# Two graph layers gather rows and sum them on TensorE: table rows stored as three bf16 parts, each sum made of three bf16 matmuls

## The chip, the cores and the metric

The kernel runs on 1 core of a Trainium2 chip. The metric is the device time of one launch in microseconds (us), lower is better. Engines: TensorE (PE; its weight loads are listed apart as PEld), VectorE (DVE), ScalarE (ACT), GpSimd (POOL), and SyncE (SP), which here issues DMAs and passes semaphores on. Each engine runs its own instruction stream in order; they meet at semaphores.

## What is computed

One layer of a graph network with 6250 nodes of 256 features and 100000 edges (sorted by `dst`), then a linear attention and a mixture of experts:

```python
xn = _layernorm(x)
# twice (W1, then W2): for every edge a row of the source node is added to the row of dst
xw  = x @ W
out = segment_sum(xw[src] * (dis[src] * dis[dst])[:, None], dst) + b   # plus the node's own row
h   = elu(out)
x = x + gnn(xn) + linear_attention(xn)
x = x + moe(_layernorm(x))           # 8 experts, top 2
```

The norm is split: a table in DRAM holds `dis[src] * row`, so that a sum over edges is a sum of table rows, scaled by `dis[dst]` afterwards.

## The kernel before, in words

The program is a row of phases with a barrier between them; each builds its own instruction streams, unrolled. Those that matter here:

- **prep** (to about 92 us). At its end 49 tiles of 128 nodes are scaled by DVE (`SCALE_V`) and ACT (`SCALE_A`) into `acc`, and SP writes them to DRAM, `table[0]`, in 7 chunks of 7 tiles.
- **l0** and **l1**, one for each graph layer. 782 tiles of 128 sorted edges meet 49 tiles of 128 destination nodes in 833 **steps**; a step is one tile of edges against one tile of nodes. `gathers` on POOL issues one indirect DMA for each tile of edges (128 table rows of 256 floats, 1 KB each) into a ring `rows` of 32 slots. `tiles_here` on SP waits for a tile's landing, raises `here`, then waits until the tile 16 places earlier has been summed (`summed`) and raises `freed`, for which POOL waits when its ring is full. `four_selects` on DVE makes 0/1 matrices for four steps at once. `step_sum` on PE multiplies one such matrix with the slot's rows into one of 4 PSUM banks, and `step_add` on DVE adds the bank to `acc`. PE may be 4 steps ahead of DVE's adds (`PSB`). Per 4 steps PE and DVE each load four words (tile counts, block offsets) into registers. Between the steps, `between(i, k)` puts other work in 49 rounds of 16 steps: the projections and context of the attention in l0, its output and the splitting of the expert weights in l1.
- **c0**, between l0 and l1: 25 pairs of node tiles are transposed, multiplied with W1 and passed through elu; POOL scales the result into `acc`, and SP writes each pair to `table[1]`. `slots` runs a software pipeline in which slot n does another stage for pair n, n-1, n-2.
- after l1: the second conv, the router, and the expert phase from about 2645 us, in which PE is busy over 90% of the time.

Of the kernel before, what the change touches and what calls it, by code (L numbers as in the profile page):

```python
# [14 lines left out]
P = 128  # L15
# [11 lines left out]
DX = D + 4  # L27
CODE = 1 << 13
# [30 lines left out]
XCH = 7  # L59
# [10 lines left out]
def gps_layer(nc, x, src, dst, wqkv, wproj, bproj, gw1, gb1, gw2, gb2, wr, br, wide, vectors, out):  # L70
# [37 lines left out]
    table = [dram(f"rows_layer{i}", [n * P, D], F32) for i, n in enumerate((NT, 2 * PAIRS))]  # L108
# [16 lines left out]
    with whole, nc.allow_non_contiguous_dma("a few columns of one word"):  # L125
# [231 lines left out]
        with ExitStack() as ph:  # L357
# [3 lines left out]
            before = sb(ph, "before", [P, SG, SG * P], BF16)  # L361
# [4 lines left out]
            rows_i = sb(ph, "rows_i", [P, 2, SG, P], I32)  # L366
            rows_b = sb(ph, "rows_b", [P, SG, P], BF16)
            rows_f = sb(ph, "rows_f", [P, SG, P])
            z_i = sb(ph, "z_i", [P, STEPS - 1], I32)
            hi_i = sb(ph, "hi_i0", [P, STEPS - 1], I32)  # L370
            lo_b = sb(ph, "lo_b", [P, STEPS - 1], BF16)
            hi_b = sb(ph, "hi_b", [P, STEPS - 1], BF16)
            hi_hot = sb(ph, "hi_hot", [P, HI, STEPS - 1], BF16)
# [3 lines left out]
            cnt_s = sb(ph, "cnt_s", [P, SCOL, GP], BF16)  # L377
# [15 lines left out]
            SCALE_V, SCALE_A = (0, 2, 4, 6), (1, 3, 5)  # L393
# [7 lines left out]
            with nc.Block() as block:  # L401
                @block.sync
                def _(sp):
# [28 lines left out]
                    for c in range(XIN):  # L432
                        sp.wait_ge(sem("scaled_v"), (c + 1) * len(SCALE_V))
                        sp.wait_ge(sem("scaled_a"), (c + 1) * len(SCALE_A))
                        sp.dma_start(table[0][c * XCH * P:(c + 1) * XCH * P, :].rearrange("(t p) d -> p t d", p=P),
                                     accv[:, c * XCH:(c + 1) * XCH, :]).then_inc(sem("tab0"), 16)
                    sp.wait_ge(sem("tab0"), XIN * 16)

                @block.gpsimd
                def _(pool):  # L440
                    pool.wait_ge(sem("copy_d"), 32)
                    for g in range(SG):
                        pool.wait_ge(sem("t_i"), g + 1)
                        at = bass.IndirectOffsetOnAxis(ap=t_i[:, g:g + 1], axis=0)
                        pool.indirect_dma_start(rows_i[:, 0, g, :], None, e_dst_rows, at).then_inc(sem("rows_d"), 16)
                    pool.wait_ge(sem("counted"), 2)
                    pool.memset(acc[:, NT * D:BLOCKS * D], 0.0).then_inc(sem("acc_tail"), 1)

                @block.vector
                def _(v):  # L450
# [92 lines left out]
                    v.wait_ge(sem("by"), 2)  # L543
                    for c in range(XIN):
                        for k in SCALE_V:
                            i = c * XCH + k
                            v.tensor_scalar(accv[:, i, :], node[:, i, :], by_x[:, i:i + 1], by_1[:, i:i + 1], ALU.mult, ALU.add
                                            ).then_inc(sem("scaled_v"), 1)

# [54 lines left out]
                def _(a):  # L604
# [22 lines left out]
                    a.activation(deg[:, :], ps_deg, ACT.Sqrt, bias=ones[:, 0:1]).then_inc(sem("std"), 1)  # L627
                    a.wait_ge(sem("by"), 2)
                    for c in range(XIN):
                        for k in SCALE_A:  # L630
                            i = c * XCH + k
                            a.activation(accv[:, i, :], node[:, i, :], ACT.Identity, scale=by_x[:, i:i + 1], bias=by_1[:, i:i + 1]
                                         ).then_inc(sem("scaled_a"), 1)

# [299 lines left out]
        with ExitStack() as ph:  # L934
            ctx_name[0] = "c0"
            work = sb(ph, "work0", [P, 10, 2 * D])
            sc, aggt, zz, ez, hh = conv_views(work)
            bk = banks(ph, 5)
            ps_t, ps_z, ps_m = bk[0:2], bk[2:4], bk[4]
            with nc.Block() as block:  # L940
                @block.sync
                def _(sp):
                    def body(n, q, has):
                        if has(2):
                            sp.wait_ge(sem("c_u0"), n - 1)
                            sp.dma_start(table[1][bass.ds((n - 2) * 2 * P, 2 * P), :].rearrange("(h p) d -> p h d", p=P),
                                         pair(accv, n - 2)).then_inc(sem("tab1"), 16)
                    slots(sp, body)
                    sp.wait_ge(sem("tab1"), PAIRS * 16)

                @block.gpsimd
                def _(pool):
# [6 lines left out]
                    slots(pool, body)  # L959
# [11 lines left out]
                def _(a):  # L971
                    a.wait_ge(sem("ctx_w"), 1)
                    a.activation(ctx_q[:, :, :].rearrange("p c o -> p (c o)"), ps_m[:, :], ACT.Copy).then_inc(sem("ctx_s"), 1)
                    conv_scalar(a, 0)

                @block.vector
                def _(v):
                    slots(v, lambda n, q, has: conv_vector(v, 0, n, q, has))


        with ExitStack() as ph:
            ctx_name[0] = "l1"
            rows = sb(ph, "rows1", [P, ROWS, D])
            rows_flat = rows[:, :, :].rearrange("p r d -> p (r d)")
            sel = sb(ph, "sel1", [P, SELS, P])
# [698 lines left out]
```

## Time and profile before

| | |
|---|---|
| device time, median of 3 runs | 3353.7 us (3351.02 to 3356.55) |
| span of the profiled execution | 3317.0 us |
| prep's table write ends, first gather of l0 | about 92 us, 93.9 us |
| steps of l0 (first to last add) | 98.0 to 1257 us |
| c0 | about 1258 to 1323 us |
| steps of l1 | 1331 to 2487 us |
| PE / DVE / ACT / POOL busy | 71% / 53% / 19% / 59% of the span |

The span runs from the first to the last instruction on the core; the device time has some 37 us more around it (3353.7 - 3317.0, if the profiled execution was a usual one). Times inside the trace are counted from the span's start. The spans of PE records are modelled, so what PE has really finished is read from the engines that wait for it.

### The profile page before, as it was taken

How to read it: one execution, taken by the hardware profiler on the slowest of the kernel's cores; microseconds unless marked ns; L12 is line 12 of the kernel's file. 1: busy time of each engine (PE TensorE's matmuls, PEld its weight loads, DVE VectorE, ACT ScalarE, POOL GpSimd, SP SyncE). 2: the span in 40 equal slices, each digit the busy share in tenths (PEclk: the TensorE clock that was granted, in tenths of full speed). 3: DMA queues.
4: the chain of work that ended last, by engine and by line, in shares of the span. 5: the costliest groups of instructions: out<-in, count | busy, mean ns of one | idle time of the engine just before them, and what ended most of it. 6: DMA issues, size and time to landing. Idle time of an engine off the chain costs nothing. (4 is left out here: it accounts for less than half of the span.)

```text
span 3317.0 us, 45225 instructions
## 1 busy us (share of the span) xinstructions
PE 2369.2 (71%) x10847; PEld 1754.6 (53%) x10847; DVE 1747.8 (53%) x4268; ACT 619.3 (19%) x1318; POOL 1965.4 (59%) x2107
## 2 busy tenths in 40 slices
PE   3366766666776678356666566666669499999998
PEld 2244444444444446234444344434448399999997
DVE  6144444444444456245444455555556666676666
ACT  2000000000000005000000011110006444444443
POOL 1566666666666653766666666666644155555554
PEclk9777888888877879677777877787789599999999
DMA  6333333333333322444444445444431455555551
GB/s 170 114 94 88 93 90 90 92 91 92 89 93 88 89 77 80 122 138 139 141 147 140 140 146 148 146 145 144 144 92 63 170 185 148 148 148 151 148 149 20
DMA packets 177902, 397.25 MB, mean 120 GB/s; under 512 B 42393, under 2 KB 96570, under 8 KB 169514
## 3 DMA queue, kind: packets, MB, share of 16 engines
q0 software_dynamic: 96800, 233.29, 26.7%
q1 hardware_dynamic: 50926, 103.38, 8.7%
q10 hardware_dynamic: 30012, 58.67, 5.2%
q8 instruction: 68, 1.11, 0.1%
q14 instruction: 96, 0.79, 0.1%
HBM read 322.87 MB, written 75.01 MB: 120 GB/s over the span
## 5 line engine op out<-in xcount | busy, mean ns | idle before, releaser
L644 POOL DMA_INDIRECT rows<-rows_layer,srcs x1564 | 1538.3, 984 | 762.3 <-issue 382.0
L705 PE MATMUL l_bank<-rows,sel 128*128 x3332 | 1191.5, 487 | 638.8 <-issue 246.1
L695 DVE TENSOR_TENSOR acc<-acc,l_bank 128x256 f32 x1666 | 698.9, 419 | 1233.1 <-remote 546.7
L705 PEld LDWEIGHTS l_bank<-rows,sel 128*128 128x128 f32 x3332 | 700.3, 235 | 1013.3 <-issue 482.7
L1638 PE MATMUL ps_y<-whl,hhi 128*128 128x512 f32 x896 | 320.8, 398 | 0.0
L1594 POOL DMA_INDIRECT out<-ys,g_sum x112 | 179.9, 1606 | 200.5 <-DVE ys L1550 175.2
L673 DVE TENSOR_TENSOR sel<-iota_n,dloc 128x512 f32<-128x512 f32 x418 | 286.4, 686 | 20.1 <-issue 20.1
L1509 ACT ACTIVATE hr<-ffn_bank,vec 128x256 f32<-128x256 f32 x448 | 212.7, 475 | 374.2 <-PE ffn_bank L1450 336.8
L1448 PE MATMUL ffn_bank<-xh,whl 128*128 128x256 f32 x896 | 252.2, 281 | 2.4 <-DVE xl L1524 2.4
L1449 PE MATMUL ffn_bank<-xl,whl 128*128 128x256 f32 x896 | 252.0, 281 | 0.0
L1450 PE MATMUL ffn_bank<-xh,whl 128*128 128x256 f32 x896 | 251.9, 281 | 0.0
L1640 PE MATMUL ps_y<-whl,hlo 128*128 128x256 f32 x896 | 250.0, 279 | 0.0
L1533 DVE TENSOR_TENSOR hlo<-hr,hhi 128x256 fp32r<-128x256 f32 x448 | 191.1, 427 | 15.4
L830 PE MATMUL l_bank<-w_qkv,xt 128*128 128x512 f32 (+1 forms) x392 | 172.2, 591 | 37.3 <-issue 31.5
L1638 PEld LDWEIGHTS ps_y<-whl,hhi 128*128 128x128 f32 x896 | 168.0, 188 | 37.6
L1448 PEld LDWEIGHTS ffn_bank<-xh,whl 128*128 128x128 f32 x896 | 169.6, 189 | 5.2 <-DVE xl L1524 2.8
L1450 PEld LDWEIGHTS ffn_bank<-xh,whl 128*128 128x128 f32 x896 | 169.6, 189 | 0.0
L1449 PEld LDWEIGHTS ffn_bank<-xl,whl 128*128 128x128 f32 x896 | 169.4, 189 | 0.0
L1640 PEld LDWEIGHTS ps_y<-whl,hlo 128*128 128x128 f32 x896 | 168.1, 188 | 0.0
L1565 POOL DMA_INDIRECT xr<-rows_x,g_row x112 | 115.9, 1034 | 63.2 <-POOL g_row L1561 44.4
L830 PEld LDWEIGHTS l_bank<-w_qkv,xt 128*128 128x128 f32 x392 | 88.9, 232 | 120.1 <-issue 105.9
L768 ACT ACTIVATE xt<-l_bank 128x256 f32<-128x256 f32 x49 | 18.8, 383 | 644.3 <-remote 420.0
(273 smaller groups left out, 2208.3 us busy)
## 6 DMA issues: line engine op xcount, KB each, us to landing
whl<-w_hi SPq DMA_DIRECT2D x32, 1024.0 KB
whl<-w_lo SPq DMA_DIRECT2D x32, 1024.0 KB
rows<-rows_layer,srcs POOLq DMA_INDIRECT x1564
w_qkv<-wide ACTq DMA_DIRECT2D x49, 335.0 KB
w_hi<-whi ACTq DMA_DIRECT2D x49, 335.0 KB
w_lo<-wlo ACTq DMA_DIRECT2D x49, 335.0 KB
rows_layer<-acc SPq DMA_DIRECT2D x25, 256.0 KB, 2.1
rows_x<-acc SPq DMA_DIRECT2D x7, 910.0 KB
```

Source lines behind the costliest of these rows:

```text
L644: pool.indirect_dma_start(rows[:, (n + 1) % ROWS, :], None, table[layer], bass.IndirectOffsetOnAxis(ap=srcs[:, n:n + 1], axis=0)).then_inc ...
L673: v.tensor_tensor(sel[:, s % SELS:s % SELS + FOUR, :], iota_n[:, None, :].to_broadcast([P, FOUR, P]), dloc[:, s:s + FOUR, None].to_broadca ...
L695: v.tensor_tensor(to, to, step_bank(s), ALU.add).wait_op(sem(f"summed{layer}"), s + 1, "sem-ge").then_inc(sem(f"added{layer}"), 1)
L705: t.matmul(step_bank(s), sel[:, s % SELS, :], rows_flat[:, bass.ds(slot * D, D)], start=True, stop=True).wait_op(sem(f"here{layer}"), t.to ...
L830: ins = t.matmul(to[:, 0:n], xt[:, c, :], w_qkv[:, c, lo:lo + n], start=(c == 0), stop=(c == KC - 1))
L1448: t.matmul(to, a[0], b[0], start=first, stop=False)
L1449: t.matmul(to, a[0], b[1], start=False, stop=False)
L1450: return t.matmul(to, a[1], b[0], start=False, stop=last)
L1509: a.activation(hr[:, m % 4, :], ps_h[m % 4][:, 0:TS], ACT.Gelu, bias=vec[q][:, O_B1 + m:O_B1 + m + 1]).then_inc(sem("e_g"), 1)
L1533: v.tensor_tensor(hl[q][:, m, :], hr[:, m % 4, :], hh[q][:, m, :].bitcast(F32), ALU.subtract).then_inc(sem("e_hs"), 1)
L1638: t.matmul(ps_y[:, h, :, :], hh[q][:, m, h * P:(h + 1) * P], whl[q][:, :, at], start=(m == 0), stop=False)
L1640: ins = t.matmul(ps_y[:, h, 0, :], hl[q][:, m, h * P:(h + 1) * P], wh[q][:, at], start=False, stop=(m == HC - 1))
```

## The change

The table in DRAM no longer holds 256 floats a row but 3 x 256 bf16 values, 1.5 KB: `hi = bf16(row)`, `mid = bf16(row - hi)`, `lo = bf16(row - hi - mid)`. The select matrices are bf16 too, and a step's sum is three accumulating bf16 matmuls. In prep and in c0 the parts are made before each table write: ACT makes `hi` and `mid`, DVE the first remainder, POOL `lo`; three part buffers rotate, each with its own semaphore of the write that reads it, and two buffers of the remainder. Prep's temporary buffers are carved out of one block so that the parts fit, and one tile of seven moves from ACT's to DVE's share of the scaling.

```diff
-    table = [dram(f"rows_layer{i}", [n * P, D], F32) ...
+    table = [dram(f"rows_layer{i}", [n * P, DP], BF16) ...      # DP = 3 * D
@@ step_sum, on PE
-            t.matmul(step_bank(s), sel[:, s % SELS, :], rows_flat[:, bass.ds(slot * D, D)], start=True, stop=True
-                     ).wait_op(sem(f"here{layer}"), t.to_reg(here), "sem-ge").then_inc(sem(f"summed{layer}"), 1)
+            t.matmul(step_bank(s), sel[:, s % SELS, :], rows_flat[:, bass.ds(slot * DP, D)], start=True, stop=False
+                     ).wait_op(sem(f"here{layer}"), t.to_reg(here), "sem-ge")
+            t.matmul(step_bank(s), sel[:, s % SELS, :], rows_flat[:, bass.ds(slot * DP + D, D)], start=False, stop=False)
+            t.matmul(step_bank(s), sel[:, s % SELS, :], rows_flat[:, bass.ds(slot * DP + 2 * D, D)], start=False, stop=True
+                     ).then_inc(sem(f"summed{layer}"), 1)
@@ l0 and l1
-            rows = sb(ph, "rows0", [P, ROWS, D])
-            sel = sb(ph, "sel0", [P, SELS, P])
+            rows = sb(ph, "rows0", [P, ROWS, DP], BF16)
+            sel = sb(ph, "sel0", [P, SELS, P], BF16)
@@ prep, per chunk c of 7 tiles; ACT (its scaling of the chunk comes first)
+                        if c >= 3:
+                            a.wait_ge(sem(f"tab0_{c % 3}"), c // 3 * 16)
+                        a.activation(part[c % 3][:, :, 0, :], accv[:, c * XCH:(c + 1) * XCH, :], ACT.Copy).then_inc(sem("part_hi"), 1)
+                        if c >= 1:
+                            middle(a, c - 1)       # waits rest(c-1), mid = Copy(rest)
@@ prep, DVE and POOL
+                        v.tensor_tensor(rest[c % 2], accv[...], part[c % 3][:, :, 0, :], ALU.subtract)
+                        pool.tensor_tensor(part[c % 3][:, :, 2, :], rest[c % 2], part[c % 3][:, :, 1, :], ALU.subtract)
@@ c0, POOL, slot n (the product of pair n-2 stands ahead of it)
+                        if has(5):
+                            m = n - 5
+                            pool.wait_ge(sem("c_mid"), m + 1)
+                            if m >= 3:
+                                pool.wait_ge(sem(f"tab1_{m % 3}"), m // 3 * 16)
+                            pool.tensor_tensor(part[m % 3][:, :, 2, :], rest[m % 2][:, :, :], part[m % 3][:, :, 1, :], ALU.subtract
+                                               ).then_inc(sem("c_lo"), 1)
@@ c0, ACT, slot n
+                        if has(3):
+                            m = n - 3
+                            a.wait_ge(sem("c_u0"), m + 1)
+                            if m >= 3:
+                                a.wait_ge(sem(f"tab1_{m % 3}"), m // 3 * 16)
+                            a.activation(part[m % 3][:, :, 0, :], pair(accv, m), ACT.Copy).then_inc(sem("c_hi"), 1)
+                        if has(4):
+                            m = n - 4
+                            a.wait_ge(sem("c_r"), m + 1)
+                            a.activation(part[m % 3][:, :, 1, :], rest[m % 2][:, :, :], ACT.Copy).then_inc(sem("c_mid"), 1)
@@ c0, DVE, slot n (after its work for pairs n-1 and n-2)
+                        if has(3):
+                            m = n - 3
+                            v.wait_ge(sem("c_hi"), m + 1)
+                            v.tensor_tensor(rest[m % 2][:, :, :], pair(accv, m), part[m % 3][:, :, 0, :], ALU.subtract
+                                            ).then_inc(sem("c_r"), 1)
```

How the change moves instructions on PE, in the middle of l0's steps. Before, a step is an address computation, its register operation with the wait, and one matmul (`sel` is the select matrix, `rows` the ring):

```order
L700 REGISTER_ALU
L705 ISA
L705 MATMUL l_bank<-rows,sel 128x256
L700 REGISTER_ALU
L705 ISA
L705 MATMUL l_bank<-rows,sel 128x256
```

In the changed kernel at the same place:

```order
L745 REGISTER_ALU
L750 ISA
L750 MATMUL l_bank<-rows,sel 128x256
L752 ISA
L752 MATMUL l_bank<-rows,sel 128x256
L753 ISA
L753 MATMUL l_bank<-rows,sel 128x256
```

A step now has three matmuls, each with a register operation of its own for its offset in the ring; still one address computation and one signal.

ACT in the middle of c0, one slot before (L871 scales the next pair, L880 copies the transposed pair out of PSUM, L884 is the exponential of elu):

```order
L871 ACTIVATE work<-acc,dis 128x256 x2
L880 ACTIVATE work<-c_bank 128x512
L884 ACTIVATE work<-work 128x512
```

One slot of the changed kernel:

```order
L919 ACTIVATE work<-acc,dis 128x256 x2
L928 ACTIVATE work<-c_bank 128x512
L932 ACTIVATE work<-work 128x512
L1039 ACTIVATE part<-acc 128x2x256
L1043 ACTIVATE part<-rest 128x2x256
```

The two part-making copies stand behind the exponential, and ahead of the next slot's scaling.

## Rows read from the trace of the kernel before

**Rows 1.** Groups of instructions on POOL in l0: busy, mean | idle before, by what ended it

```profile
L644 POOL DMA_INDIRECT rows<-rows_layer,srcs x782 | 772.3, 988 | 392.3 <-issue 187.2 <-SPq L666 173.6 <-POOLq L85 31.3
```

**Rows 2.** The same for POOL in l1

```profile
L644 POOL DMA_INDIRECT rows<-rows_layer,srcs x782 | 765.9, 979 | 370.0 <-issue 194.9 <-SPq L666 171.6 <-POOLq L940 3.2
```

**Rows 3.** Who waited for whom, SP's own queue, l0: us, times, longest

```profile
SPq L666 <- PE l_bank L705: 365.4, 288, 5.3
SPq L660 <- DMA rows<-rows_layer,srcs: 8.1, 5, 3.5
```

**Rows 4.** DVE in order of time, first round of l0: start, us, what [idle before]

```profile
117.91 0.42 DVE L695 TENSOR_TENSOR acc<-acc,l_bank 128x256 f32 x1 [3.36 <-remote]
...
122.81 0.42 DVE L695 TENSOR_TENSOR acc<-acc,l_bank 128x256 f32 x1 [3.88 <-remote]
...
158.51 1.53 DVE L695 TENSOR_TENSOR acc<-acc,l_bank 128x256 f32 x3 [17.89 <-remote]
```

**Rows 5.** POOL in order of time, the same stretch

```profile
158.78 0.95 POOL L644 DMA_INDIRECT rows<-rows_layer,srcs  x1 [7.02 <-SPq L666]
```

**Rows 6.** DVE in order of time, a later round of l0

```profile
457.61 0.42 DVE L695 TENSOR_TENSOR acc<-acc,l_bank 128x256 f32 x1 [1.82 <-remote]
460.42 0.42 DVE L695 TENSOR_TENSOR acc<-acc,l_bank 128x256 f32 x1 [2.40 <-remote]
462.63 0.42 DVE L695 TENSOR_TENSOR acc<-acc,l_bank 128x256 f32 x1 [1.78 <-PE l_bank L705]
```

**Rows 7.** POOL in order of time, the same stretch

```profile
462.90 0.95 POOL L644 DMA_INDIRECT rows<-rows_layer,srcs  x1 [2.52 <-SPq L666]
```

**Rows 8.** PE in order of time, the same stretch

```profile
457.17 1.69 PE L705 MATMUL l_bank<-rows,sel 128*128 x6
```

**Rows 9.** DVE in order of time, end of l1, all gathers landed

```profile
2476.16 0.42 DVE L695 TENSOR_TENSOR acc<-acc,l_bank 128x256 f32 x1 [0.69 <-PE l_bank L705]
...
2479.31 0.42 DVE L695 TENSOR_TENSOR acc<-acc,l_bank 128x256 f32 x1 [0.69 <-PE l_bank L705]
```

**Rows 10.** Instructions on the tile rows_i: ns min/median/max, first and last start

```profile
L445 POOL DMA_INDIRECT rows_i<-edges_dst,t_i x7: 952/952/1190, 13.9 to 21.7; - x7
...
L613 ACT ACTIVATE rows_f<-rows_i x1: 827/827/827, 38.1 to 38.1; 128x768 f32<-128x768 int32 x1
```

**Rows 11.** In order of time, the end of prep and the start of l0

```profile
69.80 10.43 ACT L632 ACTIVATE acc<-node,by,by_x 128x256 f32<-128x256 f32 x21 [0.90 <-DVE by L542]
69.80 9.13 DVE L547 TENSOR_SCALAR acc<-node,by_x,by 128x256 f32<-128x256 f32 x28
...
93.88 0.96 POOL L644 DMA_INDIRECT rows<-rows_layer,srcs  x1 [31.27 <-POOLq L85]
```

**Rows 12.** A window of prep: busy of PE, PEld, DVE, ACT, POOL, then PEclk, DMA share, GB/s

```profile
80.00:85.00 5.00, 0.00 (x0) 0.00 (x0) 0.00 (x0) 0.23 (x1) 0.00 (x0) 1.00 1.04 344
```

**Rows 13.** DMA issues of the table writes: KB each, median us to landing

```profile
rows_layer<-acc SPq DMA_DIRECT2D x25, 256.0 KB, 2.1
rows_layer<-acc SPq DMA_DIRECT2D x7, 896.0 KB, 7.9
```

**Rows 14.** In order of time, the middle of c0

```profile
1285.57 1.04 POOL L956 TENSOR_TENSOR acc<-work,dis 128x512 f32<-128x512 f32 x1 [1.13 <-DVE work L925]
...
1286.51 0.42 DVE L922 TENSOR_SCALAR work<-work 128x512 f32<-128x512 f32 x1
...
1286.83 0.62 ACT L884 ACTIVATE work<-work 128x512 f32<-128x512 f32 x1
1286.96 0.69 DVE L925 SCALAR_TENSOR_TENSOR work<-work 128x512 f32<-128x512 f32 x1
1287.35 0.90 ACT L871 ACTIVATE work<-acc,dis 128x256 f32<-128x256 f32 x2
...
1287.73 1.04 POOL L956 TENSOR_TENSOR acc<-work,dis 128x512 f32<-128x512 f32 x1 [1.13 <-DVE work L925]
...
1288.50 0.60 ACT L880 ACTIVATE work<-c_bank 128x512 f32<-128x512 f32 x1 [0.26 <-PE c_bank L896]
```

More of the change, by code:

```diff
@@ L27 @@
 DX = D + 4
+PARTS = 3
+DP = PARTS * D
 CODE = 1 << 13
@@ L107, in gps_layer @@
     tab_d = dram("step_words", [3, SG * P, 2], U16)
-    table = [dram(f"rows_layer{i}", [n * P, D], F32) for i, n in enumerate((NT, 2 * PAIRS))]
+    table = [dram(f"rows_layer{i}", [n * P, DP], BF16) for i, n in enumerate((NT, 2 * PAIRS))]
     rows_x = dram("rows_x", [1 + NT * P, DX], F32)
@@ L376, in gps_layer @@
             hi_flat = hi_hot[:, :, :].rearrange("p h s -> p (h s)")
-            cnt_s = sb(ph, "cnt_s", [P, SCOL, GP], BF16)
+            cnt_s = carve(SCOL * GP).rearrange("p (c g) -> p c g", c=SCOL)
+            part = [prep_mem[:, i * XCH * DP:(i + 1) * XCH * DP].rearrange("p (t k d) -> p t k d", t=XCH, k=PARTS) for i in range(3)]
+            rest = [prep_mem[:, 3 * XCH * DP + i * 2 * XCH * D:3 * XCH * DP + (i + 1) * 2 * XCH * D].bitcast(F32)
+                    .rearrange("p (t d) -> p t d", t=XCH) for i in range(2)]
             cnt_t = sb(ph, "cnt_t", [P, 2, 4, P], BF16)
@@ L447, in _ @@
                     pool.memset(acc[:, NT * D:BLOCKS * D], 0.0).then_inc(sem("acc_tail"), 1)
+                    for c in range(XIN):
+                        pool.wait_ge(sem("rest"), c + 1)
+                        pool.wait_ge(sem("part_mid"), c + 1)
+                        if c >= 3:
+                            pool.wait_ge(sem(f"tab0_{c % 3}"), c // 3 * 16)
+                        pool.tensor_tensor(part[c % 3][:, :, 2, :], rest[c % 2], part[c % 3][:, :, 1, :], ALU.subtract
+                                           ).then_inc(sem("part_lo"), 1)
                 @block.vector
@@ L543, in _, with remainder @@
                     v.wait_ge(sem("by"), 2)
+                    def remainder(v, c):
+                        v.wait_ge(sem("part_hi"), c + 1)
+                        if c >= 2:
+                            v.wait_ge(sem("part_mid"), c - 1)
+                            v.wait_ge(sem("part_lo"), c - 1)
+                        v.tensor_tensor(rest[c % 2], accv[:, c * XCH:(c + 1) * XCH, :], part[c % 3][:, :, 0, :], ALU.subtract
+                                        ).then_inc(sem("rest"), 1)
                     for c in range(XIN):
@@ L627, in _, with middle @@
                     a.activation(deg[:, :], ps_deg, ACT.Sqrt, bias=ones[:, 0:1]).then_inc(sem("std"), 1)
+                    def middle(a, c):
+                        a.wait_ge(sem("rest"), c + 1)
+                        a.activation(part[c % 3][:, :, 1, :], rest[c % 2], ACT.Copy).then_inc(sem("part_mid"), 1)
                     a.wait_ge(sem("by"), 2)
@@ L937, in gps_layer @@
             sc, aggt, zz, ez, hh = conv_views(work)
+            part = [sb(ph, f"part{i}", [P, 2, PARTS, D], BF16) for i in range(3)]
+            rest = [sb(ph, f"rest{i}", [P, 2, D]) for i in range(2)]
             bk = banks(ph, 5)
@@ L942, in _ @@
                 def _(sp):
[L943 to L949, printed above, removed]
+                    for m in range(PAIRS):
+                        sp.wait_ge(sem("c_lo"), m + 1)
+                        sp.wait_ge(sem("c_hi"), m + 1)
+                        sp.wait_ge(sem("c_mid"), m + 1)
+                        sp.dma_start(table[1][m * 2 * P:(m + 1) * 2 * P, :].rearrange("(h p) d -> p h d", p=P),
+                                     part[m % 3][:, :, :, :].rearrange("p h k d -> p h (k d)")).then_inc(sem(f"tab1_{m % 3}"), 16)
+                    for i in range(3):
+                        sp.wait_ge(sem(f"tab1_{i}"), len(range(i, PAIRS, 3)) * 16)
                 @block.gpsimd
```

58 lines of the change are left out of this document (39 added, 19 removed).

## The prediction

> **What bounds the kernel now.** I read the page first, then the groups and waits of the two step phases, then single rounds in order of time. The step phases l0 and l1 hold 2320 of the 3317 us of span. No engine is full in them; POOL is nearest. One gather costs POOL 0.98 to 0.99 us, and its queue adds 0.30 us before the next, so 782 gathers at full pace take 782 x 1.28 = 1003 us, while each phase takes about 1160. What POOL waits for is the rest: of the idle time ended by `freed` and by the queue's own issue (173.6 + 187.2 us in l0, 171.6 + 194.9 in l1) 782 x 0.30 = 235 us is the queue's own, which leaves 126 and 132 us in which the ring was full [rows 1, 2]. The queue of SP says who was late: it waited 365 us for PE's sums and 8 us for landings [rows 3]. So data are always there; it is the sums that come late, and POOL stands still for them.
>
> Why are they late? Not for want of PE's arithmetic. When all gathers are out, four steps take 2479.31 - 2476.16 = 3.15 us, 0.79 us a step [rows 9], well under POOL's 1.28, with DVE's adds, selects and register loads setting the pace. With gathers under way there are two regimes. In one, steps run at that pace. In the other DVE stands idle: adds come 2.8 us apart at 457.61 and 460.42 [rows 6], although PE's record has three sums at 457.17 to 458.86 [rows 8]. In the first round they come 4.9 us apart and then not at all for 18 us, while POOL issues gather after gather; POOL then stops with its ring full, idle for 7.02 us, and at 158.51 three adds run back to back [rows 4, 5]. At 462.63 the same: POOL had stopped 2.52 us before, its last gather (issued at 459.43) had landed, and four waiting sums were signalled at once [rows 6, 7]. In this regime a sum's signal is held up while gathers are in flight, and is let go when the last one has landed. I find such an episode about once a round, near 100 in all; 258 us of waits over 100 is 2.6 us, which is the pause of [rows 7]. What the hold-up is the trace does not say. It says that it isn't the length of the matmul, since sums held for microseconds are let go together.
>
> **The change, part by part.** *The sum itself.* One fp32 matmul goes, three bf16 ones come, each with its register operation. The array time gets shorter, but the fast regime is paced by DVE (worth 0 while the adds wait for DVE's own queue), and in the slow regime the hold-up is per signal, of which there is still one a step. I put the gain of the arithmetic at 0. Its bounds: all the 258 us of waits, plus the tail after the last gather (the steps still owed when the ring is full, about 30 us a phase, of which 7 would stay), 258 + 46 = 304 us gained; below, nothing.
>
> *The gather.* POOL's price does not depend on the bytes: gathers of 128 int32, 0.5 KB a row, took a median of 952 ns, as much as those of 1 KB [rows 1, 10]. So 1.5 KB adds nothing to POOL. The landing gets later by 64 KB. From the table writes (2.1 us at 256 KB, 7.9 at 896) 640 KB cost 5.8 us, which makes 64 KB 0.58 us; from the rate of a full stream, 344 GB/s, it is 0.19 us [rows 12, 13]. An episode ends with the landing of the last gather, so each gets longer by that: 100 x 0.19 to 0.58, 19 to 58 us; I take 30, nearer the lower, since the queue is empty by then. The Trainium skill ("DMA: Bandwidth & Descriptors", Anatomy of one DMA) has a fixed cost of about 2.0 us and bytes over 436 GB/s: 0.15 us more a gather, and an estimate of 15 us in place of my 30. The pause of 2.5 us agrees with its fixed cost.
>
> *PE's sequencer* has two more register operations and two more matmuls a step. Hidden while a step stays under POOL's 1.28 us; where it exceeds DVE's 0.79 it slows the catching up between episodes, and these come closer together. Bounds 0 and 67 us (episodes every 18 us instead of every 23); I take 0 here and keep the rest for the range.
>
> *Prep.* Before, ACT needs 10.43 us and DVE 9.13 for the scaling of all 49 tiles, the DMAs run at 344 GB/s and the first gather starts at 93.88 [rows 11, 12]. Now per chunk: `hi` and `mid` on ACT, 1792 elements each, by the 0.83 us of 768 [rows 10] about 1.7 us; the remainder on DVE about 2.0 (0.42 us for 256 and 0.69 for 512 elements [rows 9, 14], so 1.05 ns an element); `lo` on POOL 3.5 x 1.04 = 3.6 us [rows 14]; the write of 1344 KB 4.0 us at 344 GB/s and 2 us to its signal. Three part buffers rotate, and ACT makes `mid(c)` only after `hi(c+1)`. So from the end of `hi(c+1)`: mid 1.7, lo 3.6, write 6.0, then `hi(c+3)` 1.7: 13.0 us for two chunks. `hi(1)` ends near 76; `hi(3)` 89, `hi(5)` 102, and `hi(6)` follows `write(3)` at 107. Then `mid(6)` at 110, `lo(6)` behind `lo(5)` at 116, the last write at 122, against 92 now: **+30 us**, with 18 as the lower bound (ACT alone, 4.4 us a chunk, no wait for buffers).
>
> *c0.* A pair takes 2.16 us now (1285.57 to 1287.73), with ACT busy for 0.62 + 0.90 + 0.60 of it [rows 14]. Two copies of 0.60 make 3.3 us a pair. But a ring is closed here too. ACT's `hi(n-3)` in slot n waits for the write of pair n-6, whose `lo` POOL makes in slot n-1 behind the product of pair n-3, which in turn waits for DVE and for the exponential in slot n-1. From the end of that exponential: DVE 0.42 + 0.69, product 1.04, `lo` 1.04, the write of 384 KB about 2.5 (2.1 for 256 KB [rows 13]), hand-overs 0.6: 6.3 us to the start of `hi`. From there hi 0.6, mid 0.6, scaling 0.9, copy 0.6 and the next exponential 0.6: 3.3 us. This takes two slots, so a slot takes 4.8 us. Some 22 of 30 slots at 4.8, the others at 2.5 on average: 125 us, against 63: **+60 us**. If writes are signalled early enough the slot is 3.3 us and the sum +33.
>
> *Sum*, on the profiled span: 3317 + 0 (sums) + 30 (landings) + 30 (prep) + 60 (c0) = 3437; with the 36.7 us that lie around it (3353.7 - 3317.0) this is **3474 us**, which I round to 3470. The other phases stay as they are: the expert phase, where PE is full, uses neither table.
>
> **The rivals.** *(a) The hold-up belongs to the fp32 matmuls and goes with them.* For it: I cannot name what holds the signals, and the episodes occur in these two phases, nowhere in c0, where PE's fp32 work runs beside plain DMAs. Against it: as many held sums are let go together as are waiting. Then POOL sets the pace: 3317 - 304 + 90 + 36.7 = 3140 us, and with a tenth left 3170. It decides if more than about 90 of the 258 us of waits go, a third, since that pays for prep and c0. This one ends on the other side. *(b) It goes in part* (half of it): 3317 - 152 + 15 + 90 + 36.7 = 3307. *(c) It gets worse*: if it hangs on the time that gathers occupy the DMA engines, half as many bytes again make it half as long again, 258 x 1.5 = 387, or +129; with the 67 us for a slower catching up, up to 3317 + 129 + 67 + 90 + 36.7 = 3640; I take its middle, 3580. *(d) The rings of three do not bind*, and prep and c0 cost 18 + 33: 3435 with the landings' 30.
>
> **How the numbers follow.** The forecast with (d) as its lower end, 3420 to 3530: 0.45. (a) 0.22, 3120 to 3200. (b) 0.13, 3200 to 3340. (c) 0.16, 3530 to 3640. Near the old time, between (b) and the forecast: 0.04. A measurement of this kernel tells 0.2% (7 us) from no change. Faster: (a) and (b) with a part of the last, 0.36; same 0.02; slower 0.62. The range reaches from 3150, the middle of (a), to 3565, which leaves out a part of (a) and of (c), together under 0.2. The likeliest case's own range is 3420 to 3530.
>
> **What would show it.** Right: `freed` still ends 110 us or more of POOL's true waits in each phase; POOL's mean stays under 1.02 us; rounds with adds 2 to 5 us apart and bursts behind a pause of POOL of 2.7 us or so; the first gather at 120 to 125 us; c0's products on POOL 4.8 us apart. Wrong: if SP waits for landings rather than for PE, and the adds follow the gathers at 1.28 us, (a) holds, and my step "the hold-up is per signal" was false. If the products of c0 are 3.3 us apart, the ring was no limit. If POOL's mean rises with the bytes, each 0.1 us of it costs 156 us, which no case has.

## The result, and the profile after

The changed kernel takes **3489.15 us** (median of 4 runs, 3487.62 to 3490.59), the kernel before 3355.12 us on the same chip (4 runs, 3351.02 to 3356.94): ratio 1.0402, 95% interval 1.0387 to 1.0417. It is slower by 134 us.

The chips of this study differ more than the two kernels do. The kernel before takes 3355 us on the one of this comparison, 3320 us on two others and 3014 to 3017 us on two more. So each ratio below is against the kernel before on the same chip, and for the step phases a row is compared with a row of its own kind of chip. No chip of the experiments was used in two sessions, so "chip" here may as well mean the session on it. The trace of the kernel before that stands ahead of the prediction has a span of 3317.0 us; the executions of that kernel on the two chips of the 3320 us level have 3313 to 3323, so it belongs with them. The first and the last column of the table are of one level, the middle one is not. The last is the run after_again; its profiled execution was the slowest of four, 9 us above their median.

By stage, in us of the trace (the first gather, the last add of a step phase):

| | before | changed, first comparison | changed, a chip of the 3320 level |
|---|---|---|---|
| first gather of l0 | 93.9 | 128.3 | 129.4 |
| l0, first gather to last add | 1163.0 | 1202.6 | 1196.8 |
| c0, to the first gather of l1 | 69.3 | 134.6 | 133.6 |
| l1, first gather to last add | 1160.8 | 1189.9 | 1175.7 |
| rest | 830.0 | 831.0 | 830.5 |
| span | 3317.0 | 3486.4 | 3466.1 |

First the groups of the changed kernel's POOL, l0 and then l1, with the busy time, the mean, and the idle time before by what ended it; they answer to [rows 1, 2].

```profile
L689 POOL DMA_INDIRECT rows<-rows_layer,srcs x782 | 772.2, 988 | 408.3 <-SPq L711 214.0 <-issue 186.6 <-POOLq L87 7.4
L689 POOL DMA_INDIRECT rows<-rows_layer,srcs x782 | 760.6, 973 | 402.9 <-SPq L711 216.0 <-issue 183.1 <-POOLq L990 3.5
```

A gather of 1.5 KB rows costs POOL 988 and 973 ns, as much as one of 1 KB. By the prediction's way of counting (idle ended by `freed` and by issue, less 235 us of the queue's own), 166 + 164 = 330 us are waits for a full ring, against 258 in the trace of before, which is of another level. In after_again, of the same level, they are 313 us, 55 more. (The expectations below take 238 us for the queue, and so have 251 and 323 where this text has 258 and 330.)

SP's own queue in l0, from 120 to 1290 us (us, times, longest), which answers to [rows 3]: the sums are late, as before, and landings are not what it waits for.

```profile
SPq L711 <- PE l_bank L753: 466.3, 256, 8.7
SPq L711 <- remote: 266.3, 83, 8.7
...
SPq L705 <- DMA rows<-rows_layer,srcs: 6.9, 3, 3.8
```

The profiles of chips with waits record only a part of the semaphore events: 5768 landing events of gathers in the trace of before, where 1564 gathers make 16 each, and about all of them in before_again. So who released SP is known in part there, and a wait ended by an unrecorded event may be put down to "remote". SP's own instructions do not hang on that. In l0 of before it stood for 779 us ahead of L666, the wait for a sum, and for 92 us ahead of L660, the wait for a landing; on a chip without waits (before_again) it is 38 and 771. The sums were late.

The page's groups of the three matmuls, and of their first weight load:

```profile
L750 PE MATMUL l_bank<-rows,sel 128*128 x1666 | 578.2, 347 | 722.7 <-SPq L705 319.7
L750 PEld LDWEIGHTS l_bank<-rows,sel 128*128 128x128 bf16 x1666 | 199.3, 120 | 989.8 <-SPq L705 522.5
L752 PE MATMUL l_bank<-rows,sel 128*128 x1666 | 589.3, 354 | 8.9 <-issue 8.8
L753 PE MATMUL l_bank<-rows,sel 128*128 x1666 | 588.5, 353 | 5.5 <-issue 5.5
```

The fp32 matmul stood in the trace as two records a step. The records overlap, so their means do not add up. Counted once, PE was busy with the sums for 573 + 618 us in the two phases of before and for 459 + 543 in those of after_again, 0.72 and 0.60 us a step, although the granted clock over the phases fell from 0.80 and 0.74 to 0.73 and 0.64. The arithmetic did get shorter, by 190 us in all, and the phases still got longer.

The end of prep in order of time (start, us, what, idle before), which answers to [rows 11]. First ACT's high parts:

```profile
88.25 1.70 ACT L675 ACTIVATE prep_mem<-acc 128x1792 bf16<-128x1792 f32 x1 [4.78 <-DMA rows_layer<-prep_mem]
...
101.83 1.70 ACT L675 ACTIVATE prep_mem<-acc 128x1792 bf16<-128x1792 f32 x1 [4.96 <-DMA rows_layer<-prep_mem]
```

DVE's scalings in the same stretch:

```profile
79.30 8.22 DVE L577 TENSOR_SCALAR acc<-node,by_x,by 128x256 f32<-128x256 f32 x5
...
89.38 1.69 DVE L577 TENSOR_SCALAR acc<-node,by_x,by 128x256 f32<-128x256 f32 x5
```

DVE's remainder of the last chunk:

```profile
110.20 5.28 DVE L571 TENSOR_TENSOR prep_mem<-acc,prep_mem 128x1792 f32<-128x1792 f32 x1 [3.57 <-POOL prep_mem L468]
```

POOL's low parts, and the first gather of l0:

```profile
78.28 8.12 POOL L468 TENSOR_TENSOR prep_mem<-prep_mem 128x1792 bf16<-128x1792 f32 x2 [15.11 <-ACT prep_mem L663]
...
117.33 3.57 POOL L468 TENSOR_TENSOR prep_mem<-prep_mem 128x1792 bf16<-128x1792 f32 x1 [3.74 <-issue]
128.26 0.97 POOL L689 DMA_INDIRECT rows<-rows_layer,srcs  x1 [7.35 <-POOLq L87]
```

ACT's high part waits twice, for 4.8 and 5.0 us, for a part buffer's write. Five scalings on DVE take 1.69 us by themselves and 8.22 beside two of POOL's subtractions. The last remainder waits 3.57 us for POOL, since there are two buffers of it, and then takes 5.28 us, against 2.01 where POOL is idle.

The middle of c0 in order of time, which answers to [rows 14]. POOL:

```profile
1396.47 1.04 POOL L1007 TENSOR_TENSOR acc<-work,dis 128x512 f32<-128x512 f32 x1 [2.56 <-DVE work L973]
1397.46 1.15 POOL L1015 TENSOR_TENSOR part<-rest,part 128x512 bf16<-128x512 f32 x1
1401.18 1.04 POOL L1007 TENSOR_TENSOR acc<-work,dis 128x512 f32<-128x512 f32 x1 [2.56 <-DVE work L973]
```

DVE, from the remainder of one pair to the last step of the next:

```profile
1398.75 0.69 DVE L1056 TENSOR_TENSOR rest<-acc,part 128x512 f32<-128x512 f32 x1 [2.36 <-POOL part L1015]
1399.36 0.68 DVE L965 TENSOR_TENSOR work<-c_bank,b_g 128x512 f32<-128x512 f32 x1
1399.96 0.42 DVE L970 TENSOR_SCALAR work<-work 128x512 f32<-128x512 f32 x1
1400.41 0.69 DVE L973 SCALAR_TENSOR_TENSOR work<-work 128x512 f32<-128x512 f32 x1
```

ACT's high part:

```profile
1401.12 0.63 ACT L1039 ACTIVATE part<-acc 128x512 bf16<-128x512 f32 x1 [1.81 <-DMA rows_layer<-part]
```

The products are 1401.18 - 1396.47 = 4.71 us apart (4.54 on average over all 25), against 2.16 before. Two rings are closed here: ACT's high part waits for a part buffer (three of them), and DVE's remainder waits for POOL's low part two pairs back (two rest buffers).

### The profile page after: what moved, and what is told of

It reads as the page before. It is cut to its first block and busy times, and to the rows that moved or that the text cites. A ratio compares the mean times of both kernels' runs of the same rounds, so it can differ in the third digit from the quotient of the medians.

```text
span 3486.4 us, 52130 instructions
## 1 busy us (share of the span) xinstructions
PE 2318.2 (66%) x12513; PEld 1677.3 (48%) x12513; DVE 1795.5 (52%) x4307; ACT 665.9 (19%) x1375; POOL 2016.0 (58%) x2139
## 5 line engine op out<-in xcount | busy, mean ns | idle before, releaser
L750 PE MATMUL l_bank<-rows,sel 128*128 x1666 | 578.2, 347 | 722.7 <-SPq L705 319.7
L750 PEld LDWEIGHTS l_bank<-rows,sel 128*128 128x128 bf16 x1666 | 199.3, 120 | 989.8 <-SPq L705 522.5
L752 PE MATMUL l_bank<-rows,sel 128*128 x1666 | 589.3, 354 | 8.9 <-issue 8.8
L753 PE MATMUL l_bank<-rows,sel 128*128 x1666 | 588.5, 353 | 5.5 <-issue 5.5
L718 DVE TENSOR_TENSOR sel<-iota_n,dloc 128x512 bf16<-128x512 f32 x418 | 286.3, 685 | 19.2 <-issue 19.2
L878 PE MATMUL l_bank<-w_qkv,xt 128*128 128x512 f32 (+1 forms) x392 | 210.9, 701 | 60.2 <-issue 30.5
L752 PEld LDWEIGHTS l_bank<-rows,sel 128*128 128x128 bf16 x1666 | 187.6, 113 | 80.4 <-issue 27.3
L753 PEld LDWEIGHTS l_bank<-rows,sel 128*128 128x128 bf16 x1666 | 192.4, 115 | 68.3 <-issue 9.9
L878 PEld LDWEIGHTS l_bank<-w_qkv,xt 128*128 128x128 f32 x392 | 102.4, 275 | 159.4 <-issue 120.0
L1528 PEld LDWEIGHTS ffn_bank<-xh,whl 128*128 128x128 f32 x896 | 170.2, 190 | 5.2 <-DVE xl L1604 2.8
```

What stands on the lines that cost most here:

```text
L718: v.tensor_tensor(sel[:, s % SELS:s % SELS + FOUR, :], iota_n[:, None, :].to_broadcast([P, FOUR, P]), dloc[:, s:s + FOUR, None].to_broadca ...
L878: ins = t.matmul(to[:, 0:n], xt[:, c, :], w_qkv[:, c, lo:lo + n], start=(c == 0), stop=(c == KC - 1))
L1528: t.matmul(to, a[0], b[0], start=first, stop=False)
```

## The experiments

### The kernel before, profiled again

No edit.

> The kernel before, profiled a second time. The device time of the changed kernel lies 1.7 us above the span of its profile (3488.1 against 3486.4), that of the kernel before 36.7 us above its own (3353.7 against 3317.0). Theory: the profiled execution of before was a quick one, and a second profile has a span of 3340 to 3355, most of the 25 to 35 us in the two step phases. Rival: the gap belongs to this kernel, and the span is again 3315 to 3320.

It ran in 3011.56 us, span 3009.7, on a chip where the kernel before has a median of 3014.16 us (7 runs). Neither theory foresaw a chip 10% quicker. Its POOL in l0 and l1:

```profile
L644 POOL DMA_INDIRECT rows<-rows_layer,srcs x782 | 759.7, 971 | 269.3 <-issue 217.6 <-POOLq L85 31.3 <-SPq L666 20.4
L644 POOL DMA_INDIRECT rows<-rows_layer,srcs x782 | 769.1, 984 | 241.1 <-issue 202.5 <-SPq L666 35.3 <-POOLq L940 3.2
```

Issue and `freed` together are 238 us in either phase, which is the queue's own 235: no wait for a full ring. SP's waits from 200 to 1050 us:

```profile
SPq L660 <- DMA rows<-rows_layer,srcs: 637.0, 579, 3.2
SPq L666 <- PE l_bank L705: 0.3, 1, 0.3
```

Here SP waits for landings and not for sums. The step phases take 1004.2 and 1012.9 us, the 1003 us that the prediction has for 782 gathers at full pace, and all other stages are as in the trace of before (93.3, 68.9, 830.4 us). So the hold-up, 3317 - 3010 = 307 us of this kernel, is there on some chips and not on others. Also, the device time is only 1.9 us over the span of the same execution: nothing like 37 us lies around a span. The first trace must be from a chip of another level than the times beside it.

### One matmul of the three

```diff
-            t.matmul(step_bank(s), sel[...], rows_flat[:, bass.ds(slot * DP, D)], start=True, stop=False
-                     ).wait_op(sem(f"here{layer}"), t.to_reg(here), "sem-ge")
-            t.matmul(... slot * DP + D ..., start=False, stop=False)
-            t.matmul(... slot * DP + 2 * D ..., start=False, stop=True).then_inc(sem(f"summed{layer}"), 1)
+            t.matmul(step_bank(s), sel[...], rows_flat[:, bass.ds(slot * DP, D)], start=True, stop=True
+                     ).wait_op(sem(f"here{layer}"), t.to_reg(here), "sem-ge").then_inc(sem(f"summed{layer}"), 1)
```

> The changed kernel with the first of the three bf16 matmuls alone; the middle and low parts are made, written and gathered as before but left out of the sums. Theory (a step's pace is set by sums being held while gathers are in flight, not by the length of the matmuls): 3470 to 3490, within 20 us of the changed kernel. Rival (the three matmuls, three weight loads and the PE's sequencer set the pace of a step): two matmuls and two weight loads less are 0.5 to 0.9 us per step, so both step phases fall to what GpSimd can gather, 1003 us each, and the time is 3490 - 2 x 160 = 3170.

On the same chip, without waits: 3105.56 us (3101.63 to 3111.09), ratio 1.0307 (1.029 to 1.0325). The step phases take 999.2 and 1011.2 us, POOL's pace. It could not tell the theories apart, so it was repeated:

> The same kernel as one_matmul (middle and low parts left out of the sums), for a chip on which the kernel before takes about 3320 to 3355 us, with waits for a full ring in its step phases. Theory (the waits are a hold-up that hangs on the gathers in flight and not on the matmuls): the waits stay at 280 us or more, ratio to before 1.035 to 1.042. Rival (the hold-up comes with TensorE's load): two thirds of the matmuls gone, most of the waits go, and the ratio falls below 1.0. If the chip is one without the waits (before near 3014 us), the ratio is again 1.03 and nothing is told.

On a chip of the 3320 level (before 3319.64 us): 3396.75 us, ratio 1.0232 (1.0215 to 1.0249). POOL in l0 and l1:

```profile
L689 POOL DMA_INDIRECT rows<-rows_layer,srcs x782 | 774.6, 991 | 360.7 <-issue 206.7 <-SPq L711 139.2 <-remote 7.4
L689 POOL DMA_INDIRECT rows<-rows_layer,srcs x782 | 763.8, 977 | 362.3 <-issue 213.8 <-SPq L711 136.0 <-remote 8.9
```

111 + 115 = 226 us of waits are left (and 16 us more that the profile puts down to "remote"), with one short matmul a step and 1155.7 + 1145.8 us of phases, against 1196.8 + 1175.7 with three. The ratio lies between my two numbers: the hold-up stays, with or without the other two matmuls, but these two cost 41 + 30 = 71 us, where I had expected nothing. The 71 rest on the slowest execution of after_again. The medians of the two kernels are 3458.58 - 3396.75 = 62 us apart, and the phases of six_parts and four_rests, the same in l0 and l1, are 65 and 60 us longer than here: 60 to 71 us.

The granted clock is not what makes the waits: it was 0.63 in l0 and 0.50 in l1 of one_matmul, which has none, and 0.63 and 0.53 here.

### Longer rows with the fp32 matmul

```diff
+DW = D + D // 2
-    table = [dram(..., [n * P, D], F32) ...]
+    table = [dram(..., [n * P, DW], F32) ...]
...
-            rows = sb(ph, "rows0", [P, ROWS, D])
+            rows = sb(ph, "rows0", [P, ROWS, DW])
```

The table is written in two DMAs a chunk, columns 0 to 255 and 256 to 383; the matmul reads the first 256.

> The kernel before (one fp32 matmul, no parts) with table rows of 384 words instead of 256: 1.5 KB per row as in the changed kernel, the last 128 words a copy of the row's first and in no sum. Theory (the 69 us by which the step phases of the changed kernel are longer come from the bytes of a gather): the step phases lengthen by 50 to 70 us in sum, writing the longer rows costs some us more, 3405 to 3435. Rival (they come from the matmuls): 3355 to 3375.

On the chip without waits: 3038.18 us, ratio 1.0075 (1.0058 to 1.0092), of which 12.5 us is the later first gather (105.8), and 10.4 + 1.2 us the phases. The median gather lands 3.1 us after its issue, against 2.8 in before_again, so the bytes do make each landing 0.3 us later (the chips with waits have too few events recorded to say). Again at the level with waits:

> The same kernel as wide_fp32 (rows of 1.5 KB, one fp32 matmul, the last 128 words in no sum), for a chip with the waits. Theory (the additional waits of the changed kernel, 56 to 72 us, come with the bytes of a gather): waits of 300 to 325 us against 251, ratio to before 1.02 to 1.03. Rival (they come with the matmuls): waits of 250 us, ratio 1.007 as on the chip without waits.

3334.80 us against 3319.64, ratio 1.0048 (1.0031 to 1.0065). POOL in l0 and l1:

```profile
L646 POOL DMA_INDIRECT rows<-rows_layer,srcs x782 | 775.2, 991 | 406.6 <-issue 182.7 <-SPq L668 180.1 <-POOLq L86 42.9
L646 POOL DMA_INDIRECT rows<-rows_layer,srcs x782 | 762.0, 974 | 376.1 <-issue 198.0 <-SPq L668 173.3 <-POOLq L942 3.9
```

128 + 136 = 264 us of waits, 6 more than in the trace of before; the phases take 1165.9 and 1160.1 us, +2.9 and -0.7. The rival holds: the phases are not measurably longer for half as many bytes again.

### Rows of the high part alone

```diff
-    table = [dram(..., [n * P, DP], BF16) ...]
+    table = [dram(..., [n * P, D], BF16) ...]
...
-                                     part[c % 3].rearrange("p t k d -> p t (k d)")).then_inc(...)
+                                     part[c % 3][:, :, 0, :]).then_inc(...)
```

> As one_matmul, with table rows of the high part alone, 0.5 KB each, both when written and when gathered (middle and low parts are made but neither written nor summed). Theory (hold-up grows with the bytes in flight, 251 us at 1 KB, 307 to 323 at 1.5 KB): waits of 180 to 200 us, 110 to 120 us less than one_matmul on the same chip. Rival 1 (it hangs on the number of gathers and their rows): the same waits as one_matmul. Rival 2: it goes altogether below some load, and the step phases take 1003 to 1015 us each.

3390.44 us, ratio 1.0207 (1.019 to 1.0224), beside one_matmul_2 on the same chip. POOL in l0:

```profile
L689 POOL DMA_INDIRECT rows<-rows_layer,srcs x782 | 771.2, 986 | 364.5 <-issue 212.7 <-SPq L711 143.3 <-POOLq L87 5.2
```

By the same count 121 + 120 = 241 us are waits, against 226, where my theory had 110 to 120 less. The phases take 1158.3 and 1144.7 us, against 1155.7 and 1145.8 with rows three times as long. Rival 1 holds, my theory falls: the hold-up does not shrink with the bytes, from 1.5 to 0.5 KB a row.

### The changed kernel again, and the two rings of c0

No edit in the first; in the others, for c0 alone, part buffers 3 to 6 and rest buffers 2 to 4:

```diff
-            part = [sb(ph, f"part{i}", [P, 2, PARTS, D], BF16) for i in range(3)]
-            rest = [sb(ph, f"rest{i}", [P, 2, D]) for i in range(2)]
+            part = [sb(ph, f"part{i}", [P, 2, PARTS, D], BF16) for i in range(6)]
+            rest = [sb(ph, f"rest{i}", [P, 2, D]) for i in range(4)]
```

> The changed kernel again, beside the kernel before on the same chip. In the first comparison the step phases of both kernels held 251 us (before) and 323 us (changed) of waits for a full ring; on the chip of the first four experiments no step phase of any kernel held one, and before took 3014 us. Theory (the waits belong to the chip or its state, and the change costs the longer preparation and the longer conversion phase by itself): on a chip like the second, changed minus before is 34 + 65 us plus at most 10, so 3110 to 3125 against 3014; on one like the first, 3490 against 3355. Rival (the waits come and go by kernel): the two kernels' step phases change independently, and the difference lies outside 95 to 140 us.

3458.58 us against 3319.54, ratio 1.0417 (1.04 to 1.0434), so +139 us, near the 135 us that the theory has for a chip with waits, and just inside the 95 to 140 beyond which the rival would hold; the level of the first comparison did not come back.

> The changed kernel with six part buffers instead of three and four rest buffers instead of two in the conversion phase between the layers. Theory (the slot of 4.7 us is the ring through these buffers, and both bind): the pitch of the GpSimd products falls from 4.5 us to 3.0 to 3.5 us, and the time by 25 to 35 us, to 3455. Rival 1 (the engines' own work in a slot fills it): no change, 3489. Rival 2 (the DMA writes set the pace): pitch stays above 4 us, at most 10 us less.

> The changed kernel with six part buffers instead of three, the two rest buffers as they are. With both rings widened the pitch of the conversion phase fell from 4.5 to 3.3 us and the phase from 134 to 102.5 us. Theory (both rings bind in parallel): six part buffers alone bring at most 5 us, since the rest ring (rest, middle, low, two slots apart) holds the pitch at 4.3 to 4.7 us. Rival 1 (the part ring binds): the phase falls to 103 us and the time by 30 us. Rival 2 (each brings half): 15 us.

> The changed kernel with four rest buffers instead of two in the conversion phase, three part buffers as they are. Six part buffers alone shortened the phase from 133.6 to 129.3 us, both rings together to 102.5 us. Theory (two rings of equal length bind in parallel): four rest buffers alone give 3 to 8 us, the phase takes 126 to 131 us. Rival (the rest ring is the one that binds): the phase falls to 103 to 108 us.

| | c0, us | pitch of the products | ratio to before |
|---|---|---|---|
| 3 parts, 2 rests (after_again) | 133.6 | 4.52 | 1.0417 |
| 6 parts, 2 rests | 129.3 | 4.43 | 1.0415 (1.0397 to 1.0434) |
| 3 parts, 4 rests | 128.3 | 4.30 | 1.0425 (1.0406 to 1.0444) |
| 6 parts, 4 rests | 102.5 | 3.27 | 1.0237 (1.022 to 1.0255), on the chip without waits |

The absolute 3455 us expected of both_rings was meant for a chip with waits; it ran where before takes 3014 us, in 3085.91 us. What carries over is the phase, which did not depend on the chip: with both rings closed it took 133.4 us in one_matmul, on the chip of both_rings, and 133.6 in after_again. So it is -4 and -5 us for one ring, -31 us for both. Two rings bind in parallel. With both open, POOL in order of time:

```profile
1181.91 1.42 POOL L1007 TENSOR_TENSOR acc<-work,dis 128x512 f32<-128x512 f32 x1 [0.63 <-DVE work L973]
1183.29 1.33 POOL L1015 TENSOR_TENSOR part<-rest,part 128x512 bf16<-128x512 f32 x1
1185.25 1.42 POOL L1007 TENSOR_TENSOR acc<-work,dis 128x512 f32<-128x512 f32 x1 [0.63 <-DVE work L973]
```

DVE of the same kernel:

```profile
1183.65 1.53 DVE L973 SCALAR_TENSOR_TENSOR work<-work 128x512 f32<-128x512 f32 x1
1185.10 0.68 DVE L1056 TENSOR_TENSOR rest<-acc,part 128x512 f32<-128x512 f32 x1
```

And a window of its c0: busy us of PE, PEld, DVE, ACT and POOL, then the granted clock, the DMA share and GB/s:

```profile
1165.00:1230.00 65.00, 44.06 (x212) 32.98 (x212) 64.35 (x79) 53.63 (x108) 52.88 (x39) 0.98 0.32 121
```

The pitch is 3.34 us now, and DVE is the next bound, busy for 64.35 of 65 us: its L973 takes 1.53 us where it takes 0.69 in the changed kernel, when it starts while POOL's subtraction (1183.29 to 1184.62) still runs.

### Plain loads in place of gathers

```diff
-                pool.indirect_dma_start(rows[:, (n + 1) % ROWS, :], None, table[layer], ...).then_inc(...)
+                pool.dma_start(rows[:, (n + 1) % ROWS, :], table[layer][n % NT * P:(n % NT + 1) * P, :]).then_inc(...)
```

In sp_plain the same load stands on SyncE's queue, which waits for `summed` before it and for the landing of the load three back behind it, and POOL's `gathers` is left out.

> The kernel before, with SyncE loading each tile's rows by a plain DMA of 128 neighbouring table rows (the edge indices are left out of the loads; GpSimd idles in the step phases), at most four in flight. What is measured is whether TensorE's signals still come late: ScalarE's copy of a transposed tile (xt) starts 0.04 us after the transposes' end on the chip without waits, and at the median 2.4 us after it in the kernel before on a chip with them. Theory (signals of TensorE are held by the indirect gathers that GpSimd makes): on a chip of the second kind the delay is 0.04 us, no sum comes late, and the time is at least 250 us below before. Rival (rows arriving in on-chip memory hold them, whoever asks): the median delay stays at 2 us or more and the step phases keep a large part of their 1160 us. On a chip of the first kind (before near 3014 us) nothing is told of it.

> The kernel before, with GpSimd issuing a plain DMA of 128 neighbouring table rows where it issued a gather (the indices are left out); all else as before, up to 32 tiles ahead. Theory (the hold-up goes with the indirect gather's own way of making its descriptors): the delay of xt is 0.04 us, the waits for a full ring are gone or short, and the phases follow the issue rate. Rival (any DMA that GpSimd issues holds the signals): median delay 2 us or more as in the kernel before.

Both fell on a chip without waits (before 3016.76 us), so the question that they were made for stays open. They took 2514.92 us (ratio 0.8345, 0.8323 to 0.8367) and 2502.64 us (0.8294, 0.8278 to 0.831). POOL of pool_plain in l0:

```profile
L644 POOL DMA_DIRECT2D rows<-rows_layer x782 | 416.3, 548 | 340.6 <-SPq L665 302.1 <-POOLq L85 31.1 <-issue 5.7
```

What they do tell: without the edge indices the phases take 752 and 759 us (sp_plain) or 753 and 748 (pool_plain), first to last add, 0.9 us a step, against 1000 and 1008 in before_again. On such a chip some 250 us of each phase are what 782 indirect gathers cost over plain loads; what paces POOL then is a full ring again, 302 us of it in l0.

## Why the prediction was right

The forecast of 3470 us was 0.5% below the result. Prep and c0 were right in size and in their main mechanism. That the sum came out this near is in part luck: two terms of the step phases were wrong in opposite directions, and an addend that does not exist stood in for the difference of two chips. Term by term, against the trace of before and after_again, both of the 3320 level:

- **Prep, +30.** Measured +35.5 (93.9 to 129.4), and +34.4 in the first comparison. The ring through three part buffers is seen in ACT's two waits for the write, and `hi(3)` and `hi(5)` end at 90.0 and 103.5, near the 89 and 102 foreseen. The rest is a cost that I had not counted: DVE beside POOL, above all the last remainder, which waits for POOL and then takes 5.28 us. The first gather came at 128.3, after the 120 to 125 named as a sign.
- **c0, +60 at a slot of 4.8 us.** Measured +64 to +65, with a slot of 4.71. The ring that I named binds, but so does a second of the same length, through the rest buffers, which I missed. Opening each alone, and then both, showed it. Rival (d), no ring binds, is out, though its 3.3 us a pair is what both open rings give.
- **Sums, 0.** This is one of the two mis-sized terms, with "PE's sequencer ... I take 0 here". One short bf16 matmul in place of the fp32 one gains 24.5 us (one_matmul_2 against wide_fp32_2, same chip: -10.2 and -14.3); two more matmuls a step cost 60 to 71, about the upper bound of 67. Net +36 to +47. That the hold-up is not in the length of the matmul was right: 190 us less of busy PE went with phases that are 36 to 49 us longer.
- **Landings, +30.** Mis-sized the other way. A landing does come 0.3 us later, but "An episode ends with the landing of the last gather, so each gets longer by that" is false: wide_fp32_2 puts it at +2 us, and half_row, at a third of the bytes, has the same phases. The episodes were miscounted too: POOL pauses for over 0.5 us 187 times in the trace of before, 1.6 us on average, where I had 100 of 2.6. Even the 15 us that the prediction estimates from the Trainium skill ("DMA: Bandwidth & Descriptors", Anatomy of one DMA) are more than is seen. The two errors partly cancel: 0 + 30 was forecast, 33.8 + 14.9 = 49 found in the stage table, and 39 by the medians (139 less 35.5 and 64.3).
- **Gathers on POOL, 0.** Right: 988 and 973 ns against 988 and 979 [rows 1, 2].
- **What lies around the span, 36.7.** False. It is 1.7 us in the changed kernel (3488.13 against 3486.4). The 37 us were the difference between a trace and times of two chips. Since the result was measured on the slower one, the addend stood in for that difference. On the 3320 level the forecast without it is 3437 us, and 3458.6 were measured.
- **Rivals (a) and (b).** Out: with PE's work cut to one bf16 matmul, 226 of 258 us of waits are still there, so less than 90 go. What went is the fp32 matmul of the sums; the attention's own stayed in l0 and l1, and no run is without them. Rival (c), a hold-up in proportion to the bytes, is out by half_row; its other half, a slower catching up, fits what was found.

**What the hold-up is.** That the sums come late and that this paces POOL was right for that trace, and the rows below show it on an instruction that has nothing to do with gathers. ScalarE copies a tile (xt) that PE has just transposed. PE's transposes in after_again, on a chip with waits:

```profile
473.31 0.63 PE L869 MATMUL l_bank<-ident,xc 128*128 128x128 f32 x2
497.19 0.63 PE L869 MATMUL l_bank<-ident,xc 128*128 128x128 f32 x2
```

ACT's copies that wait for them:

```profile
475.70 0.38 ACT L816 ACTIVATE xt<-l_bank 128x256 f32<-128x256 f32 x1 [14.10 <-remote]
501.87 0.38 ACT L816 ACTIVATE xt<-l_bank 128x256 f32<-128x256 f32 x1 [18.91 <-remote]
```

PE's transposes in before_again, on the chip without:

```profile
200.13 0.62 PE L821 MATMUL l_bank<-ident,xc 128*128 128x128 f32 x2
...
219.76 0.38 PE L821 MATMUL l_bank<-ident,xc 128*128 128x128 f32 x2
```

And ACT's copies there:

```profile
200.79 0.38 ACT L768 ACTIVATE xt<-l_bank 128x256 f32<-128x256 f32 x1 [13.61 <-PE l_bank L821]
...
220.18 0.38 ACT L768 ACTIVATE xt<-l_bank 128x256 f32<-128x256 f32 x1 [12.74 <-PE l_bank L821]
```

There the copy starts 0.04 us after the transposes' end, in 49 of 49 tiles. On the other chip it starts 1.76 and 4.05 us after it. The median over the 49 tiles is 4.0 us in after_again, 2.4 in the trace of before, 3.8 in wide_fp32_2 and 0.7 in one_matmul_2 and half_row. So what PE has done in its records is known to others late, a transpose as well as a sum, on some chips alone. With three matmuls a step more of the 49 copies are late by over 1 us (40) than with one bf16 matmul (23); with one fp32 matmul it is 32 in the one trace and 44 in the other.

The pauses of POOL tell more. Those over 0.5 us number 132 in one_matmul_2 and 139 in half_row, 2.1 us each on average, and 233 in after_again, 1.6 us each; the two fp32 kernels lie between, with 187 and 197. Three matmuls make the pauses more frequent and not longer, which is what a slower catching up between episodes would do.

Shown: the hold-up goes with the chip or the session on it; it stays with the sums' fp32 matmul gone; it does not shrink with the bytes. Argued only: that the catching up is what two more matmuls lengthen. Open: what holds the sums there; whether PE itself finishes late, since the ends of its records are modelled, or only its signals are late; and whether it takes indirect gathers, since the two kernels with plain loads did not meet such a chip. A rival that no run touches is the recording itself. Every trace with waits lacks most of the gathers' landing events and every trace without them has about all, so the hold-up and the loss of events go together, and every execution of the experiments has a span and a granted clock on record. Whether the kernel is slow on those chips when nothing is recorded, these runs cannot say.

No version that still computes the layer is faster than the kernel before. The widened rings take back 31 us of the 134 to 139; the preparation and the bare ACT work of the parts keep the rest, for sums that are signalled no sooner. On a chip without waits the change buys nothing in the phases (1012.0 and 1012.4 us in both_rings, 1004.2 and 1012.9 before) and costs its prep and c0 in full: 3085.9 + 31 = 3117 us, 3.4%, as an estimate from both_rings with the rings closed again.

## What to carry to other kernels

Before a faster form of an operation is bought with preparation work, look for who waits for that operation and why: here either POOL's gathers set the pace and the matmul lay beside them, or the sums were late for a reason that its form did not remove, and more matmuls a step, though shorter, made it worse. Two rings in parallel hide each other, so a buffer count is judged only when every ring through the same slot is opened. And take profile and times from the same chip: a term that explains the difference between them is otherwise an invention.

## What the runs showed of the hardware that I had not expected

- **Chips differ by 10% on one kernel.** 3355, 3320, 3320, 3014 and 3017 us for the same code; none of the experiments' chips was met in a second session, so chip and session can't be told apart. Between the two levels that were traced (spans 3317.0 and 3009.7) all of it lies in the step phases: prep, c0 and the rest agree within 1 us.
- **DVE and POOL stand in each other's way on on-chip tensors.** Five scalings take 1.69 us alone and 8.22 beside POOL's subtractions of 8.12; POOL's product takes 1.04 or 1.42 us, DVE's L973 0.69 or 1.53. The Trainium skill ("SBUF — State Buffer", SBUF: two separate sides) has DVE and GpSimd share a pair of ports as an exclusive lock, for DVE instructions in a two-port mode or with two on-chip inputs: the later one is blocked until the earlier ends. The trace agrees: two of the five scalings take 3.68 and 3.66 us and end 0.15 us after POOL's two subtractions (at 82.97 and 86.55, against 82.82 and 86.40), the other three take 0.40 us each.
- **A gather's price on POOL does not depend on its bytes.** It was 966 to 991 ns at 0.5, 1 and 1.5 KB a row; a plain DMA of 128 neighbouring rows of 1 KB cost 548 ns.
- **Fewer busy microseconds on PE, a lower granted clock and little gain.** With one bf16 matmul a step in place of the fp32 one, PE's busy time on the sums fell from 558 + 635 us (wide_fp32_2) to 244 + 287 (one_matmul_2), the granted clock from 0.82 and 0.72 to 0.63 and 0.53, and the two phases got 24.5 us shorter.
